# Gather by single banks, gathered probabilities in two parts, and a new order of steps

## The reference, cut to what matters

```python
c_kv = x @ W_dkv
I = jnp.einsum('bths,h->bts', jax.nn.relu(jnp.einsum('bthd,bsd->bths', q_i, k_i)), idx_w)
I = jnp.where(local[None], jnp.inf, I)
I = jnp.where(causal[None], -jnp.inf, I)
_, idx = jax.lax.top_k(I, kk)                       # kk = 96
key_c = (c_kv @ W_uk)[bi, idx].reshape(B_, L_, kk, N_HEAD, D_HEAD)
value = (c_kv @ W_uv)[bi, idx].reshape(B_, L_, kk, N_HEAD, D_HEAD)
...
kr_sel = (x @ W_kr)[bi, idx]
key_r = _pope(kr_sel, angles_k[None, None, :, :])
scores = (jnp.einsum('bhld,bhlkd->bhlk', q_c, k_c) + jnp.einsum('bhld,blkd->bhlk', q_r, key_r)) * scale
attn = jax.nn.softmax(scores.astype(jnp.float32), axis=-1).astype(v.dtype)
out = jnp.einsum('bhlk,bhlkd->bhld', attn, v)
...
return out @ W_out
```

## Time and profile before

| | |
|---|---|
| median of three runs | 1385.41 us (1380.8 to 1389.0) |
| the profiled execution | 1387.57 us |
| its span, first to last instruction | 1385.7 us |
| mean granted TensorE clock | 0.958 |
| TensorE busy | 1217.4 us, 88% |
| weight loads (beside the matmuls) | 847.7 us, 61% |
| VectorE busy | 906.4 us, 65% |
| ScalarE busy | 878.2 us, 63% |
| GpSimd busy | 364.9 us, 26% |
| matmuls | 11271 |
| critical chain: TensorE, VectorE, ScalarE | 52%, 20%, 18% |

### The profile page before, as it was taken

One profiled execution on the slowest core, in us unless ns is written; L12 is line 12 of the kernel. 1 busy time (PEld: TensorE's weight loads), 2 busy tenths in 40 slices (PEclk: granted clock), 3 DMA queues, 4 the chain that ended last, 5 costly groups with the idle time before them and its releaser, 6 DMA issues.

```text
span 1385.7 us, 29670 instructions
## 1 busy us (share of the span) xinstructions
PE 1217.4 (88%) x11271; PEld 847.7 (61%) x11271; DVE 906.4 (65%) x2920; ACT 878.2 (63%) x2243; POOL 364.9 (26%) x580
## 2 busy tenths in 40 slices
PE   7779988789999898888899988887998989889897
PEld 6446655556676665555667755554676656556566
DVE  3966577657475867665766677765667486666533
ACT  3426687646665777755865777764847556874573
POOL 0710232212340423310532143311324042321022
PEclk9889999999999999999999999999999988999998
DMA  8121000000120000000112000000021000000000
GB/s 304 47 79 28 2 1 1 1 5 1 55 75 21 15 2 1 1 1 5 50 24 84 4 6 1 1 1 5 2 74 56 19 17 2 1 0 1 1 1 9
DMA packets 31791, 34.82 MB, mean 25 GB/s; under 512 B 19169, under 2 KB 23713, under 8 KB 31137
## 3 DMA queue, kind: packets, MB, share of 16 engines
q1 hardware_dynamic: 31648, 32.92, 7.9%
HBM read 25.46 MB, written 7.44 MB: 24 GB/s over the span
## 4 chain that ended last, share of the span: by engine, by line
PE 52%; DVE 20%; ACT 18%; issue 4%; DMA 1%; SPq 1%; POOL 1%; DVEq 0%; POOLq 0%; ACTq 0%
PE ps L624 4%; ACT arena L1513 4%; PE ps L1222 3%; ACT arena L1260 3%; DVE small L2049 3%; PE ps L804 3%; PE ps L1232 2%; PE ps L1213 2%; PE ps L687 2%; ACT arena L1566 2%; PE ps L1044 2%; PE ps L746 2%; PE ps L731 2%; PE ps L1118 2%; PE ps L762 2%
## 5 line engine op out<-in xcount | busy, mean ns | idle before, releaser
L1260 ACT ACTIVATE arena<-ps 128x512 f32<-128x512 f32 (+5 forms) x544 | 255.3, 490 | 203.9 <-PE ps L770 29.3
L2231 POOL TENSOR_TENSOR arena<-arena 128x512 f32<-128x512 f32 x64 | 81.9, 1289 | 262.0 <-DVE arena L1722 260.7
L1513 ACT ACTIVATE arena<-arena,small 128x128 f32<-128x128 f32 (+1 forms) x256 | 130.2, 513 | 7.4 <-DVE small L1986 7.2
L1697 DVE CUSTOM_DVE_ANT_0 arena<-ps,mask_w_bf 128x128 f32<-128x128 f32 (+1 forms) x256 | 67.6, 320 | 83.1 <-PE ps L746 82.9
L2049 DVE TENSOR_REDUCE small<-ps 128x4 f32<-128x1024 f32 x64 | 75.4, 1219 | 29.1 <-PE ps L1118 28.8
L1910 DVE TENSOR_TENSOR gath<-ps,rank_tab 96x512 f32<-96x512 f32 x96 | 62.3, 681 | 34.5 <-PE ps L632 22.6
L1566 ACT ACTIVATE arena<-ps 128x512 f32<-128x512 f32 x128 | 66.5, 607 | 26.8 <-PE ps L1157 26.7
L1222 PE MATMUL ps<-w_experts,late 128*128 128x128 f32 x544 | 72.8, 288 | 7.2 <-DVE late L2157 6.7
L1222 PEld LDWEIGHTS ps<-w_experts,late 128*128 128x128 f32 x544 | 68.5, 200 | 15.6 <-DVE late L2157 9.5
L1460 ACT ACTIVATE arena<-arena,small 128x224 f32<-128x224 f32 (+1 forms) x128 | 56.8, 448 | 27.3 <-DVE small L1934 27.1
L2101 DVE SCALAR_TENSOR_TENSOR late<-ps,late 128x128 f32<-128x128 f32 x128 | 39.3, 354 | 52.7 <-PE ps L1222 51.4
(11 more groups left out here) (296 smaller groups left out, 2980.5 us busy)
## 6 DMA issues: line engine op xcount, KB each, us to landing
idxb<-idx_scratch SPq DMA_DIRECT2D x24, 512.0 KB, 5.2
score_scratch<-arena SPq DMA_DIRECT2D x96, 64.0 KB, 1.7
w_experts<-in_experts SPq DMA_DIRECT2D x3, 1088.0 KB, 16.2
w_wqkv<-in_wqkv SPq DMA_DIRECT2D x1, 1536.0 KB, 9.3
arena<-score_scratch SPq DMA_DIRECT2D x96, 16.0 KB, 2.0
arena<-in_x SPq DMA_DIRECT2D x8, 128.0 KB, 2.1
out_x<-late SPq DMA_DIRECT2D x8, 128.0 KB, 1.9
packed<-in_packed SPq DMA_DIRECT2D x2, 503.0 KB, 4.1
```

The costliest lines, as they stand in the source:

```text
L1260: return act.activation(dst, src, ACT.Copy)
L1513: ins = act.activation(probs, probs, ACT.Exp, bias=nb[s][:, i, h:h + 1], scale=cqs[s][:, T, hh_:hh_ + 1], accum_out=ls[s][:, i, h:h + 1])
L2231: ins = pool.tensor_tensor(own, own, turned, ALU.add)
```

## The change

Four edits. In `gather`, each group of three matmuls is now a step of its own with its own wait for the evacuation of the group two places earlier; the second pass of the last four groups stays in pairs. `turn_gathered` has two parts: tile 0 and the first half of the heads of tile 1 after the third unit's probabilities, the rest after the fourth's. The copy into `pdiag` is split by tile into two steps of four copies, both after both parts, and the product with the gathered latents into two steps that wait for one each. All orders of steps, the fillers and the lent banks are written anew: `BUSY` sums to 528 matmuls in 110 places, before 437 in 66.

The places below show the order on an engine, before and then now. In the names, `arena0` and `arena1` are the streams' memories, `hot_ring` and `idxb` the one-hot tables, `late` the experts'. Lines of the new kernel are up to ten higher from L1443 on, and one to four off before.

```diff
@@ STEPS_IN_TURN, BUSY and LENT: all of their rows are new; one of each @@
-    "sp": ("051202110216031122061821021101210311011102162103110221041823"),
+    "sp": ("07130216011102220511011721031121041101110116210111022104110111011623"),
...
-BUSY = [("b0h303000000000700000133000000060000000000000006000000000010040h030080000000000000000000000000600500000000j00000"
-LENT = ("5645031413020123342234301267403074213230546701324031373230237030147604453203546701233456233273470132507600320102"
+BUSY = [("e0h4fu00000002000000001000000000c000000001000002200000b000004004020300000100000000000000008000000002000000000000"
+LENT = ("2302746017403740433723475337266453365645012330121032342475370170565763313302107474015377743132475607130167760102"
...
@@ -162,8 +161,8 @@
     "gather_act": ["gsc_ready", "gathT_ready"] * 3,
     "gather_dve": ["hot_ready"] * 3 + ["gath_evac"] * 12,
     "zeroed": ["late_masked", "pdiag_zero", "m_zero", "v_zero"],
-    "proj_mm": (["xg_turned", "a_out", "og_mm", "a_out"] + (["f_o"] + ["f_g"] * 2 + ["f_a"] * 2 + ["f_down"]) * 2),
-    "proj_act": ["pdiag_ready", "og_ready"] + ["f_gelu"] * 4,
+    "proj_mm": (["xg_turned", "xg_turned", "a_out", "og_mm", "og_mm", "a_out"] + (["f_o"] + ["f_g"] * 2 + ["f_a"] * 2 + ["f_down"]) * 2),
+    "proj_act": ["pdiag_ready", "pdiag_ready", "og_ready"] + ["f_gelu"] * 4,
     "proj_dve": (["a_added", "x_updated", "shifted", "shifted"]
                  + ["shifted"] * 2 + ["f_hidden"] * 2 + ["shifted"] * 2
                  + ["shifted"] * 2 + ["f_hidden"] * 2 + ["x_updated"] * 2),
@@ -607,18 +606,18 @@
             def gather(p):
 
                 n = p // 2
-                yield
-                claim([0, 1], ("gath_evac", 2 * p + 2))
-                if p == 0:
-                    pe.wait_ge(*at("kv_split", 5))
-                    pe.wait_ge(*at("qa_copied", 2))
-                    pe.wait_ge(*at("qb_copied", 2))
-                else:
-                    pe.wait_ge(*at("gath_evac", 2 * p))
-                if p == 0:
-                    keep_busy(bank[0][:, 0:L])
-                pe.wait_ge(*at("hot_ready", n + 1))
                 for g in (2 * p, 2 * p + 1):
+                    yield
+                    claim([g % 2], ("gath_evac", g + 1))
+                    if g == 0:
+                        pe.wait_ge(*at("kv_split", 5))
+                        pe.wait_ge(*at("qa_copied", 2))
+                        pe.wait_ge(*at("qb_copied", 2))
+                        keep_busy(bank[0][:, 0:L])
+                    if g % 4 == 0:
+                        pe.wait_ge(*at("hot_ready", n + 1))
+                    if g >= 2:
+                        pe.wait_ge(*at("gath_evac", g - 1))
                     part = slice(512 * (g % 4), 512 * (g % 4) + 512)
                     for i in range(3):
                         last = mm(bank[g % 2][0:GF, :], m.kv_part[i][:, 0, :], hot[n][:, part], start=(i == 0), stop=(n < 2 and i == 2))
@@ -719,14 +718,16 @@
                                   start=False, stop=True)
                 last.then_inc(*one("u_pv"))
 
-            def turn_gathered():
-
-                yield
-                claim([1], ("pdiag_ready", 1))
-                pe.wait_ge(*at("u_prob", 4))
-                for h in range(H):
-                    for T in range(2):
-                        rows_, to, n = (slice(LW, P), 0, 16) if T == 0 else (slice(0, P), 16, 32)
+            def turn_gathered(part):
+
+                yield
+                if part == 0:
+                    claim([1], ("pdiag_ready", 2))
+                    pe.wait_ge(*at("u_bias", 4))
+                pe.wait_ge(*at("u_prob", 3 + part))
+                for T, half in (((0, 0), (0, 1), (1, 0)), ((1, 1),))[part]:
+                    rows_, to, n = (slice(LW, P), 0, 16) if T == 0 else (slice(0, P), 16, 32)
+                    for h in range(4 * half, 4 * half + 4):
                         for t in range(GP):
                             last = mm(bank[1][RANKS * t:RANKS * t + RANKS, NG * h + to:NG * h + to + n],
                                       m.probs_a[T][rows_, h, keys(T):], ident[rows_, rows_.start + t::GP], start=True, stop=True)
@@ -936,8 +937,8 @@
                         yield from att_scores(i)
                     if 0 < i < 4:
                         yield
-                    if i == 5:
-                        yield from turn_gathered()
+                    if i >= 4:
+                        yield from turn_gathered(i - 4)
                     if i >= 2:
                         yield from att_values(i - 2)
                     if 0 < i < 5:
@@ -956,12 +957,15 @@
                 yield
                 claim([3], ("og_ready", 1))
                 keep_busy(bank[3][:, 0:L])
-                pe.wait_ge(*at("pdiag_ready", 1))
-                for j in range(NG):
-                    q, jj = j % 4, j // 4
-                    last = mm(bank[3][32 * q:32 * q + 32, 32 * jj:32 * jj + 32], m.gathT[:, j, :],
-                              m.pdiag[:, j, :, :].rearrange("p t h -> p (t h)"), start=True, stop=True)
-                last.then_inc(*one("og_mm"))
+                for T in range(2):
+                    if T == 1:
+                        yield
+                    pe.wait_ge(*at("pdiag_ready", T + 1))
+                    for j in range(*((0, 16) if T == 0 else (16, NG))):
+                        q, jj = j % 4, j // 4
+                        last = mm(bank[3][32 * q:32 * q + 32, 32 * jj:32 * jj + 32], m.gathT[:, j, :],
+                                  m.pdiag[:, j, :, :].rearrange("p t h -> p (t h)"), start=True, stop=True)
+                    last.then_inc(*one("og_mm"))
                 yield
                 claim(range(4), ("x_updated", 1))
                 keep_busy(bank[1][:, 0:L])
@@ -1439,12 +1443,18 @@
                 for i in range(6):
                     yield
                     if i == 5:
-                        act.wait_ge(*at("xg_turned", 1))
-                        act.wait_ge(*at("pdiag_zero", 1))
-                        for t in range(GP):
-                            part = slice(RANKS * t, RANKS * t + RANKS)
-                            ins = copy(m.pdiag[part, :, t, :], bank[1][part, 0:H * NG].rearrange("p (h j) -> p j h", j=NG))
-                        ins.then_inc(*one("pdiag_ready"))
+                        for T in range(2):
+                            if T == 1:
+                                yield
+                            act.wait_ge(*at("xg_turned", 2))
+                            if T == 0:
+                                act.wait_ge(*at("pdiag_zero", 1))
+                            g0, g1 = (0, 16) if T == 0 else (16, NG)
+                            for t in range(GP):
+                                part = slice(RANKS * t, RANKS * t + RANKS)
+                                src = bank[1][part, 0:H * NG].rearrange("p (h j) -> p j h", j=NG)
+                                ins = copy(m.pdiag[part, g0:g1, t, :], src[:, g0:g1, :])
+                            ins.then_inc(*one("pdiag_ready"))
                     if i >= 2:
                         u = i - 2
                         yield
@@ -1466,7 +1476,7 @@
                         yield from turned_out(0, i - 1, m.PTa[(i - 1) % 2])
                     yield
                 yield
-                act.wait_ge(*at("og_mm", 1))
+                act.wait_ge(*at("og_mm", 2))
                 copy(m.og, bank[3][:, 0:3 * P].rearrange("p (j t h) -> p j t h", t=GP, h=H)).then_inc(*one("og_ready"))
                 yield
                 yield from ln_square(1)
```

81 lines of the change are left out of this document (40 added, 41 removed).

## The result

The changed kernel took 1375.44 us, the median of 16 runs (1371.93 to 1383.92), and the kernel before 1383.75 us, the median of 16 (1375.12 to 1389.34), on the same chip. The ratio is 0.9948, 95% interval 0.9929 to 0.9966: a little over half a per cent faster, 7.2 us of 1384. The profiled execution of the changed kernel took 1376.06 us, its span is 1374.3 us and its mean granted clock 0.979.

What follows compares the result with a forecast made beforehand. TensorE, busy 88%, was taken as the bound, with 168.3 us idle plus lost clock to win. -4 +0 +3 -8 -2 = -11 on 1387.57 gave 1376.6; the median, 2.2 lower, gave 1374, range 1349 to 1397.

Steps and rivals of the forecast that it cites:

- gather bank by bank: Gather: each group of three matmuls waits for its own bank alone, cutting TensorE's 6.5 us of evacuation waits; -4 us.
- gathered probabilities in two parts: Transposes, pdiag copies and product: earlier transposes mostly off the path, ScalarE's extra 5.8 us hidden; 0 (-20.8 to +5.8).
- chain: Path to `xg_turned`: 48 of 64 transposes moved earlier take 2.6 us per item off it, 20.8 us over eight items.
- Fillers: Small matmuls before TensorE's waits: 91 more at 0.144 us, a quarter taken as exposed; +3 us (0 to +13.1).
- Clock: Last 326 us: 24 more fillers in the last round can hold the higher clock level; -8 us (-17.2 to +6).
- Order and start: Rewritten engine orders: stream 1 starts some 10 us later but has cover, stream 0 gains 0.8 us; -2 (-34 to +10).
- A: Rival, whole kernel: no change, one wait replaced by another, no gain of clock; 1384 us, chance 0.25.
- B: Rival, TensorE: a clearly denser order removes a fifth of its 168.3 us idle time, -34; 1351 us, chance 0.12.
- C: Rival, start: stream 1's late start isn't covered and keeps its 10 us until the end; 1395 us, chance 0.14.
- D: Rival, gather: bank-by-bank waits add short pauses that lower the clock, +13.6 us; 1399 us, chance 0.07.

Runs made afterwards that it cites:

- gather alone: Kernel before with each gather group waiting for its own bank, a step still holding a pair, old order and fillers: 1376.82 us, ratio 0.9961.
- all code in the old order: The changed kernel's four code edits with the order and fillers of the kernel before: 1384.66 us, ratio 1.0029.
- tiles apart: Kernel before with two loops exchanged, so the transposes of the gathered probabilities go tile by tile, not head by head: 1373.09 us, ratio 0.9926.
- two kernels, 7.5 and 9.5: Kernel before with tile-by-tile transposes and single-bank gather (0.9898), plus either transposes in two parts (1376.03 us, 0.9952) or copies and product cut (1377.02 us, 0.9967).
- by turns: Kernel before with the two tiles' transposes alternating one by one, 63 changes of operand height per item: 1477.85 us, ratio 1.0693.
- two small edits in the old order: Kernel before with transposes tile by tile and the gather's waits by single banks, old order: 1368.69 us, ratio 0.9898.

## Why the prediction was right, and where not

The time was right, 1374 against 1375.44 us, and so was the side; the sum of the steps was -11 against a measured -7.2. That it lies so near is in part luck: the second step was 9.4 us too favourable, the last row and the gather 4.2 and 1.4 not favourable enough, and the kernel before measured 1383.75 and not 1385.41, which covers 1.7 more. The steps, each as 1383 us times the distance of a ratio from 1 or from another, so that each is known to 4 to 6 us:

| step | predicted | measured | from |
|---|---|---|---|
| gather bank by bank | -4 (-6.5 to 0) | -5.4 | gather alone |
| gathered probabilities in two parts | 0 (-20.8 to +5.8) | +9.4 | all code in the old order, less gather alone |
| of it: changes of height | not seen | -10.2 | tiles apart |
| of it: the split | not seen | +17.0, in two halves | two kernels, 7.5 and 9.5 |
| fillers, clock and order | +3, -8, -2 = -7 | -11.2 | after, less all code in the old order |

The two parts of the second step make -10.2 + 17.0 = +6.8 and were measured together as +9.4, which is the same within what these runs can tell.

**Gather.** The size was right within its interval, the reading of the wait was not. The experiment kept each pair in one step, so what the single steps of the changed kernel add is in the last row. I said that the waits for L1920 would fall to about 2; they are 7.5. The longest answers to the one at 94.52 in the earlier trace rows:

```profile
94.62 4.48 PE L623 MATMUL ps<-hot_ring,arena 128*96 128x512 bf16 x12 [3.37 <-DVE gath L1920]
```

VectorE just before it, in the kernel after:

```profile
88.30 0.75 DVE L1899 TENSOR_SCALAR hot_ring<-idxb,packed 128x2048 bf16<-128x2048 bf16 x1 [3.64 <-DMA idxb<-idx_scratch]
88.97 0.16 DVE L1944 TENSOR_SCALAR small<-small 128x4 f32<-128x4 f32 x1
90.05 0.75 DVE L1899 TENSOR_SCALAR hot_ring<-idxb,packed 128x2048 bf16<-128x2048 bf16 x1 [0.91 <-DMA idxb<-idx_scratch]
91.36 0.75 DVE L1907 TENSOR_SCALAR idxb<-idxb,packed 128x2048 bf16<-128x2048 bf16 x1 [0.56 <-DMA idxb<-idx_scratch]
92.03 1.95 DVE L1908 TENSOR_SCALAR idxb<-idxb,packed 128x2048 bf16<-128x2048 bf16 x1
93.90 1.27 DVE L1920 TENSOR_TENSOR gath<-ps,rank_tab 96x512 f32<-96x512 f32 x2
```

The first pair of banks was full by 90.6 (L623 had started at 89.11, 1.50 long), but VectorE first waits for the second and the third transfer of the indices and builds the last three one-hot tables. The evacuation starts at 93.90 whatever TensorE's wait looks like. Waiting for one bank instead of two saves one copy of some 0.65 us, not the three that the row names. I had taken "waits for the evacuation" as "waits for the evacuation's duration".

**Two parts.** This is the step that failed. Its value was 0, and it measured +9.4, known to about 6 us: clear of 0, on the side of the upper end (+5.8) and probably over it. Two things went into it that I hadn't priced. The first is a rule of the Trainium skill that speaks for the change and that I passed over: "TensorEngine Tiling (Array Packing)", section "Key Properties", says that changing the tiling mode drains TensorE. That page of the Trainium skill gives no price and doesn't say that the pause seen here is this drain; the trace agrees with its direction, and the pauses of this case are 0.11 to 0.19 us a change. I priced the 64 transposes by their group of 3.46 us and carried it over as if three quarters of it went with three quarters of the instructions; the row said x128, with 3.46 / 128 = 27 ns, while the product beside it (L962) went at 1.03 / 96 = 11 ns. That ratio was the sign. The second is the split itself. ScalarE's copies were sized well: 12.0 + 8.6 = 20.6 us, predicted 21.2. But "ScalarE is idle a third of the time, which hides it" didn't hold, since L955 stands behind the last of them: a wait of 4.1 us that was not there, and 7.1 in the old order. Also the "chain" that the earlier part was to shorten by up to 20.8 us wasn't the path: the early transposes alone cost 7.5. In the third round's item of stream 1 the two parts stand nine microseconds apart on TensorE:

```profile
803.67 1.68 PE L732 MATMUL ps<-packed,arena 64*32 64x16 f32 x96
...
812.62 0.67 PE L732 MATMUL ps<-packed,arena 128*32 128x32 f32 x32
...
817.89 1.05 PE L966 MATMUL ps<-arena 128*32 128x32 f32 x96
```

From the end of the last transposes (813.29) to the product it is 4.6 us, before 811.34 - 804.49 = 6.9; from the first transposes to the product 14.2 us against 10.3 before.

**Fillers.** Their line was to be 76 us and is 81.2, at 0.154 us each instead of 0.144. That a quarter of it is exposed is neither right nor wrong: it depends on the order. In the new order none is, and the run is 17.3 us shorter with them (1.0073 and 0.9948); in the old one the fillers cost 0.99% (13.7 us, interval 8.3 to 18.9), about my upper end of 13.1.

**Clock.** I said 0.95 or more from 1060 us on; it is 0.97, and the busy time there fell by 14.0 us. But my reason, the 24 more fillers in that round, isn't shown. Gather alone, with the old fillers in the old order, has this in the same stretch:

```profile
1060.00:1386.00 326.00, 270.75 (x2538) 192.16 (x2536) 196.12 (x572) 198.33 (x503) 70.78 (x110) 0.97 0.03 7
```

and the tiles apart has 0.95 and 268.98 us busy, with old fillers too. So the 0.92 of the earlier trace rows was most likely this one execution's for the greater part, and so were the 14.0 us. Over the whole run the clock rose by some 0.008, an estimated 11 us, so that a gain of the order of the -8 was there, but not where I had put it. What the fillers do to the clock shows in the new order with and without them: 0.979 and 0.964 in the profiles, 0.973 and 0.963 over the executions. I had taken the clock of one execution for the kernel's.

**Order and start.** Stream 1's first projections were to start near 53 us and start at 54.21; its index load was to be issued between 82 and 86 and is at 84.29:

```profile
54.21 1.06 PE L873 MATMUL ps<-arena,packed 128*128 128x256 f32 x2
```

```profile
80.44 0.60 SPq L513 DMA_DIRECT2D idx_scratch<-arena  x1
...
84.29 1.29 SPq L524 DMA_DIRECT2D idxb<-idx_scratch  x3
```

Its search was done at 77.47 (L1888 at 77.19, 0.28 long), not 81.3, so that ten microseconds of later start became 1.0 us at the load (83.30 before), the last part of it by SyncE, whose store waited until 80.44 behind the reload of stream 0's scores (2.46 us from 77.93). The order alone, with the old fillers, costs 0.44% against the same code in the old order (1.0073 and 1.0029, intervals that overlap).

**The rivals.** A (no change, 1384) came nearest of them: the lower end of the gain is 0.34%. B (a denser order) is refuted: the idle time didn't fall (184.3 us, against 185.6 for the same code in the old order, and 201.3 in the new order with the old fillers). C (the late start) didn't decide, by the rows above: 1.0 us at the load and not 10. D (pauses bank by bank lower the clock) is refuted by gather alone: 0.968 over the executions against 0.966 beside it, and a ratio below 1; the changed kernel itself has 0.973. The rule cited for it (the Trainium skill, "TensorE: Matmul & The Clock Gate", section "A second HAM failure mode: psum-queue depth-cycling") isn't borne out by this edit.

## What to carry to other kernels

When many small matmuls of two operand heights are issued, put those of one height together, or give all of them the full height if zeros or a selection allow it; look for it by dividing a group's busy time by its count and comparing with a neighbour, since the mean of one doesn't show it. A wait for a buffer says who frees it, not why late: read the freeing engine's timeline before pricing the buffer. Fillers placed by count belong to one order, so the two are judged only together; and a low clock in one profiled execution is compared with the clocks of other executions, or with a second kernel of the same order, before a gain is put on it. Last, a change of several parts is best taken apart: here two small edits in the old order (0.9898) do better than the whole change (0.9948).

## What the hardware showed that I had not expected

A change of a matmul's operand height between 64 and 128 rows costs TensorE, in these fp32 transposes of 32 weight columns, 0.11 us when four transposes of one height lie between changes and 0.19 us when nearly every one changes; at the extreme the line of 1024 passes went from 15.67 to 111.61 us and the kernel to 1.0693. Such pauses count as busy time in the profile. Beside it the granted clock over the run fell from 0.964 to 0.929, also in the stretch from 346 to 692 us, with tiles apart and by turns:

```profile
346.00:692.00 346.00, 306.24 (x2938) 214.43 (x2937) 228.73 (x734) 238.10 (x598) 102.60 (x160) 0.99 0.08 23
```

```profile
346.00:692.00 346.00, 313.28 (x2767) 219.03 (x2768) 215.42 (x700) 217.80 (x552) 91.41 (x144) 0.94 0.07 18
```

TensorE is no less busy there (313.28 against 306.24), yet its clock is 0.94 instead of 0.99. The two kernels differ in the order of the transposes alone, so that order lowers the clock; that it does so through the pauses inside the busy time is argued and not shown.
